# Softmax weights and an index row placed in PSUM in three edge passes of a four-layer graph network

## The reference

```python
h = jnp.maximum(_layernorm(x, axis=-1), 0.0)
x = x + _L0_gnn_ref(h, ..., node_type_4, edge_type_8, src, dst)   # typed keys, queries, values
x = x + _L1_gnn_ref(h, edge_index, ...)                            # graph attention, self loops
x = x + _L2_gnn_ref(h, src, dst, weight, bias)                     # graph convolution
x = x + _L3_gnn_ref(h, src, dst, Wq, Wk, Wv, ...)                  # clipped attention, 8 heads
```

```python
a = (kw * q_e).sum(-1) * pri / sqrt_d                 # layer 0: a dot product per edge and head
amax = jax.ops.segment_max(a, dst, num_segments=n)    # layers 0 and 1
ex = jnp.exp(a - amax[dst])
denom = jax.ops.segment_sum(ex, dst, num_segments=n)
agg = jax.ops.segment_sum(msg * att[..., None], dst, num_segments=n)
```

## Time and profile before

| | us |
|---|---|
| median of 3 runs | 10693.53 |
| lowest and highest | 10691.29, 10695.21 |
| the profiled execution | 10696.8 |
| its span, first to last instruction | 10695.1 |
| POOL busy | 7984.3 (75%) |
| PE busy | 6694.1 (63%) |
| PE weight loads | 5319.6 (50%) |
| DVE busy | 5218.1 (49%) |
| ACT busy | 2509.1 (23%) |

### The profile page before, as it was taken

The page is one execution under the profiler, slowest core; times in us unless marked ns, Lnnn a source line. Parts: engine busy times, 40 slices in busy tenths (PEclk is TensorE's granted clock), DMA queues, the critical chain, the costliest instruction groups (busy, mean ns, idle before and its releaser), DMA issues. The chain is left out here.

```text
span 10695.1 us, 165052 instructions
## 1 busy us (share of the span) xinstructions
PE 6694.1 (63%) x38290; PEld 5319.6 (50%) x38291; DVE 5218.1 (49%) x13802; ACT 2509.1 (23%) x6808; POOL 7984.3 (75%) x11114
## 2 busy tenths in 40 slices
PE   4977777777756667666663333333337777777776
PEld 3656665655535555555553232232224555555554
DVE  4266666666665555555553111111114555555555
ACT  1333333333343333333333000000002111111111
POOL 0188888888848888888865666666663888888884
PEclk9966666676765555555556555565556666666667
DMA  3333333333312212222111222222222332333332
GB/s 112 148 88 88 87 87 87 87 88 88 87 46 47 46 44 46 45 46 45 44 40 46 46 46 46 47 46 46 46 46 63 87 87 87 87 87 87 87 87 63
DMA packets 379652, 731.26 MB, mean 68 GB/s; under 512 B 169770, under 2 KB 219233, under 8 KB 373126
## 3 DMA queue, kind: packets, MB, share of 16 engines
q0 software_dynamic: 251264, 621.88, 22.1%
q1 hardware_dynamic: 100762, 97.56, 2.8%
q10 hardware_dynamic: 27500, 10.39, 0.4%
HBM read 652.50 MB, written 76.88 MB: 68 GB/s over the span
## 5 line engine op out<-in xcount | busy, mean ns | idle before, releaser
L465 POOL DMA_INDIRECT edges_rows<-conv_rows,edges_idx_r x1568 | 1536.9, 980 | 773.6 <-issue 457.9
L465 POOL DMA_INDIRECT edges_rows<-gat_rows,edges_idx_r x1568 | 1562.8, 997 | 336.1 <-issue 260.1
L465 POOL DMA_INDIRECT edges_rows<-kv_typed,edges_idx_r x1568 | 1597.6, 1019 | 267.6 <-issue 263.5
L465 POOL DMA_INDIRECT edges_rows<-kv_rows,edges_idx_r x1568 | 1522.2, 971 | 271.6 <-issue 267.7
L1022 PE MATMUL edges_ps_sum<-edges_rows,edges_pick 128*128 x3520 | 763.3, 355 | 1511.7 <-issue 1386.9
L629 PE MATMUL edges_ps_sum<-edges_wv,edges_pick 128*128 128x132 f32 x7040 | 1671.9, 409 | 20.9 <-issue 13.4
L472 POOL TENSOR_TENSOR edges_pause<-edges_pause 128x56 f32<-128x56 f32 x4704 | 1599.9, 340 | 108.1 <-issue 18.1
L629 PEld LDWEIGHTS edges_ps_sum<-edges_wv,edges_pick 128*128 128x128 f32 x7040 | 1427.0, 297 | 256.6 <-issue 246.5
L1022 PEld LDWEIGHTS edges_ps_sum<-edges_rows,edges_pick 128*128 128x128 f32 x3520 | 647.9, 257 | 1627.1 <-issue 1625.7
L1120 PE MATMUL edges_ps_q<-q,edges_pick_t 128*128 x3520 | 748.7, 379 | 674.5 <-DVE edges_prod L1184 649.7
L1042 DVE TENSOR_TENSOR sums<-sums,edges_ps_sum 128x129 f32 x440 | 126.9, 288 | 1858.5 <-DMA edges_rows<-gat_rows,edges_idx_r 1486.5
(11 more groups left out here) (345 smaller groups left out, 10934.8 us busy)
## 6 DMA issues: line engine op xcount, KB each, us to landing
kv_typed<-l0pre_out SPq DMA_DIRECT2D x49, 1024.0 KB
edges_rows<-kv_typed,edges_idx_r POOLq DMA_INDIRECT x1568
edges_rows<-gat_rows,edges_idx_r POOLq DMA_INDIRECT x1568
edges_rows<-conv_rows,edges_idx_r POOLq DMA_INDIRECT x1568
edges_rows<-kv_rows,edges_idx_r POOLq DMA_INDIRECT x1568
edges_feat_r<-visit_features ACTq DMA_DIRECT2D x660, 10.0 KB
kv_rows<-l3pre_kv SPq DMA_DIRECT2D x7, 896.0 KB
edges_flag_r<-visit_flags ACTq DMA_DIRECT2D x220, 16.0 KB
```

Of the source, the lines that this page charges most:

```text
L465: pool.indirect_dma_start(rows[:, k, g * width:(g + 1) * width], None, table, bass.IndirectOffsetOnAxis(ap=idx_r[:, k, g:g + 1], axis=0)). ...
```

## The change

It has four parts. First, DVE reads the softmax weights of `weigh` from a PSUM bank `ps_weight` in passes 0, 1 and 3. ACT writes them there with an `Exp` of its own, for the whole span in passes 0 and 1 and for the visit in pass 3, after DVE has read the weights before (`wv_done`); the `Exp` into `wv` stays, since PE sums that column. Second, in pass 0 the index row for `pick_b` is copied once into a PSUM bank `ps_iota` and read from there, as pass 3 did before. Third, the banks for this come from `ps_near`: one in place of two in pass 0, with the squares two visits ahead in place of three, and two in place of three in pass 3, with the squares three ahead in place of four. Fourth, in passes 0 and 1 `ps_turn` goes: the logits are turned, and turned back, in the first 128 columns of `ps_top`, and the maxima move up behind them. `turn_logits` therefore waits for `gap_b` of the span before, and `block_max` no longer does.

```diff
@@ -513,15 +513,16 @@
-        near_banks = 2 if dot else 1
-        ps_near = [p.ps(f"ps_near{j}", [P, GE]) for j in range(near_banks)]
+        ps_near = p.ps("ps_near", [P, GE])
...
-        ps_turn, ps_top = p.ps("ps_turn", [P, 512]), p.ps("ps_top", [P, 512])
+        ps_iota, iota_done = (p.ps("ps_iota", [P, GE]), p.sem("iota_done")) if dot else (None, None)
+        ps_top, ps_weight = p.ps("ps_top", [P, 512]), p.ps("ps_weight", [P, 512])
...
-        part9 = ps_top[:, 0:9 * SG].rearrange("p (n k) -> p n k", k=9)
-        ref8 = ps_top[:, 160:160 + 8 * SG].rearrange("p (n k) -> p n k", k=8)
+        turned_top = ps_top[:, 0:P]
+        part9 = ps_top[:, P:P + 9 * SG].rearrange("p (n k) -> p n k", k=9)
+        ref8 = ps_top[:, 288:288 + 8 * SG].rearrange("p (n k) -> p n k", k=8)
...
@@ -561,18 +562,17 @@
-                    nc.tensor.transpose(ps_turn[:, 0:P], logit[:, r, :], c["ident"]).then_inc(turn_done, 1)
+                        pe.wait_ge(gap_b, w)
+                    nc.tensor.transpose(turned_top, logit[:, r, :], c["ident"]).then_inc(turn_done, 1)
...
-                    nc.tensor.transpose(ps_turn[:, P:2 * P], run[:], c["ident"]).then_inc(back_done, 1)
+                    nc.tensor.transpose(turned_top, run[:], c["ident"]).then_inc(back_done, 1)
...
-                    if known(w, 1):
-                        pe.wait_ge(gap_b, w)
...
@@ -591,11 +591,11 @@
-                    if known(u, near_banks):
-                        pe.wait_ge(pick_tb_done, u + 1 - near_banks)
+                    if known(u, 1):
+                        pe.wait_ge(pick_tb_done, u)
...
-                    mm = nc.tensor.matmul(ps_near[s % near_banks][:], c["col_feat"], near, start=True, stop=True)
+                    mm = nc.tensor.matmul(ps_near[:], c["col_feat"], near, start=True, stop=True)
...
@@ -639,7 +639,7 @@
-                    to_square, to_spread, last, ninth = (wide_at(i, k, it, d) for d in (3 if dot else 2, 1, -1, -9))
+                    to_square, to_spread, last, ninth = (wide_at(i, k, it, d) for d in (2, 1, -1, -9))
...
@@ -656,7 +656,7 @@
-                wide_visits(pe, body, -3, 10)
+                wide_visits(pe, body, -2, 10)
...
@@ -665,6 +665,9 @@
+                        if known(u, 1):
+                            act.wait_ge(wv_done, u)
+                        nc.scalar.activation(ps_weight[:, 0:SH], gap[:, s // SPAN, :], ACT.Exp).then_inc(span_weighed, 1)
...
@@ -713,12 +716,12 @@
-                        nc.scalar.activation(pick_t[:, s % 2, :], ps_near[s % near_banks][:], ACT.Relu, bias=1.0, scale=-1.0).then_inc(pick_t_done, 1)
+                        nc.scalar.activation(pick_t[:, s % 2, :], ps_near[:], ACT.Relu, bias=1.0, scale=-1.0).then_inc(pick_t_done, 1)
...
-                    nc.scalar.activation(pick_tb[:, s, :], ps_near[s % near_banks][:], ACT.Relu, bias=1.0, scale=-1.0).then_inc(pick_tb_done, 1)
+                    nc.scalar.activation(pick_tb[:, s, :], ps_near[:], ACT.Relu, bias=1.0, scale=-1.0).then_inc(pick_tb_done, 1)
...
@@ -770,7 +773,7 @@
-                                            c["iota_bf"].unsqueeze(1).broadcast_to([P, G, P]),
+                                            ps_iota[:, 0:P].unsqueeze(1).broadcast_to([P, G, P]),
...
@@ -812,8 +815,9 @@
-                    nc.vector.tensor_tensor(wv4[:, s % 3, :, :, 0:hd], vals, bcast(wv4[:, s % 3, :, :, hd], [P, G, heads, hd]),
-                                            ALU.mult).then_inc(wv_done, 1)
+                    j = s % SPAN
+                    weights = ps_weight[:, j * GH:(j + 1) * GH].rearrange("p (g h) -> p g h", g=G)
+                    nc.vector.tensor_tensor(wv4[:, s % 3, :, :, 0:hd], vals, bcast(weights, [P, G, heads, hd]), ALU.mult).then_inc(wv_done, 1)
...
@@ -832,11 +836,11 @@
-                    nc.vector.tensor_tensor_scan(run[0:SH, :], flag_r[:, r, :], ps_turn[0:SH, 0:P], -BIG, ALU.add, ALU.max).then_inc(run_done, 1)
+                    nc.vector.tensor_tensor_scan(run[0:SH, :], flag_r[:, r, :], turned_top[0:SH, :], -BIG, ALU.add, ALU.max).then_inc(run_done, 1)
...
-                    nc.vector.tensor_tensor(ends[:], ps_turn[:, P:P + SH].rearrange("p (n h) -> p n h", h=heads),
+                    nc.vector.tensor_tensor(ends[:], turned_top[:, 0:SH].rearrange("p (n h) -> p n h", h=heads),
...
@@ -966,7 +970,9 @@
+                    nc.vector.tensor_copy(ps_iota[:, 0:P], c["iota_bf"]).then_inc(iota_done, 1)
...
+                    dve.wait_ge(iota_done, 1)
...
@@ -1068,14 +1074,15 @@
-        ps_near = [p.ps(f"ps_near{j}", [P, GE]) for j in range(3)]
+        ps_near = [p.ps(f"ps_near{j}", [P, GE]) for j in range(2)]
...
+        ps_weight = p.ps("ps_weight", [P, 512])
...
@@ -1095,9 +1102,9 @@
-                    if known(u, 3):
-                        pe.wait_ge(pick_t_done, u - 2)
-                    nc.tensor.matmul(ps_near[s % 3][:], c["col_feat"], feat_r[:, s // 2 % 3, s % 2], start=True,
+                    if known(u, 2):
+                        pe.wait_ge(pick_t_done, u - 1)
+                    nc.tensor.matmul(ps_near[s % 2][:], c["col_feat"], feat_r[:, s // 2 % 3, s % 2], start=True,
...
@@ -1122,7 +1129,7 @@
-                    to_square, to_spread, third = (wide_at(i, k, it, d) for d in (4, 1, -3))
+                    to_square, to_spread, third = (wide_at(i, k, it, d) for d in (3, 1, -3))
...
@@ -1134,7 +1141,7 @@
-                wide_visits(pe, body, -4, 4)
+                wide_visits(pe, body, -3, 4)
...
@@ -1146,6 +1153,9 @@
+                        if known(u, 1):
+                            act.wait_ge(wv_done, u)
+                        nc.scalar.activation(ps_weight[:, 0:G * heads], gap[:, s % 3], ACT.Exp).then_inc(gap_weighed, 1)
...
@@ -1155,7 +1165,7 @@
-                        nc.scalar.activation(pick_t[:, s % 2, :], ps_near[s % 3][:], ACT.Relu, bias=1.0, scale=-1.0).then_inc(pick_t_done, 1)
+                        nc.scalar.activation(pick_t[:, s % 2, :], ps_near[s % 2][:], ACT.Relu, bias=1.0, scale=-1.0).then_inc(pick_t_done, 1)
...
@@ -1189,7 +1199,8 @@
-                                            bcast(wv4[:, w, :, :, hd], [P, G, heads, hd]), ALU.mult).then_inc(wv_done, 1)
+                                            bcast(ps_weight[:, 0:G * heads].rearrange("p (g h) -> p g h", g=G), [P, G, heads, hd]),
+                                            ALU.mult).then_inc(wv_done, 1)
...
```

8 lines of the change are left out of this document (4 added, 4 removed).

## The result

The change is slower where it was first measured: 11201.41 us in the median of 4 runs (11185.15 to 11213.58) against 10694.37 for the kernel before, a ratio of 1.047 with a 95% interval of 1.0455 to 1.0485. The forecast was 10435.5. Later the same kernel was faster, 10041.85 us against 10300.83, ratio 0.9744 [0.9727, 0.976], in runs in which the kernel before was faster too. Both results hold. The experiments show what differs between the two sets of runs; what makes it differ stays open.

The account below looks back on a forecast made before the run. POOL was taken to bound passes 0 and 3, the consumers pass 1. Gains of 115 + 10 + 134 - 1 = 258 us from the median of 10693.5 gave 10435.5 us, range 10350 to 10540.

Parts of the forecast that it names:

- The stretch under L772, L815 and L1191 goes: Passes 0, 1, 3: POOL no longer stretched beside these DVE instructions; 143, 33 and 134 us of POOL time.
- A PSUM operand costs DVE nothing by itself: DVE's relieved reads: price taken as nothing, from L782 beside L1191, both 0.68 us for 512 columns.
- Parts 2, 3 and 4: Prediction's numbering: added Exp 0, up to 20 us; one bank of squares less 0; shared logits bank 0 to 20.
- POOL's time saved is time of the pass: Passes 0 and 3: POOL sets their length, so its relief shortens them, by 115 and 134 us.
- What is late next: Pass 0 after the change: consumers alone need 2238 us at 4.88 a visit plus 91, against POOL's 2260.
- The charge of 28 us: Pass 0: deducted for consumer stalls reaching POOL, between nothing and 91 us, leaving a gain of 115.
- 134 stays: Pass 3: the full 134 us gain is kept, with consumers far ahead, waiting 307 us for rows.
- the ring in pass 0: Rival, chance 0.05: with one bank, squares wait for both ACT one-hots; 6.06 us a visit, 10914 us overall.
- about 0.9 us uncovered a visit: Pass 0: the uncovered ACT time per visit from which the prediction said the ring decides.
- The gathers-not-relieved rival: Chance 0.06: long gathers only coincide with L772 and L815; at most 58 and 117 us of pauses go, 10519 us.
- The sign that was set for being wrong: Pass 0: POOL's wait for L815 appearing with more than 60 us would show the prediction wrong.
- The sum: Whole kernel: 115 in pass 0, 10 in pass 1, 134 in pass 3, less 1, gives 258 us.

Follow-up runs that it names:

- e5: The changed kernel with weigh reading its weights from SBUF again and without the added Exp and its wait; 10733.38 us, ratio 1.0048.
- e6: The changed kernel with the added Exp and its wait kept, but weigh reading the weights from SBUF; 10751.16 us, ratio 1.0056.
- e1: The kernel before with only one bank of squares less and the shorter lookahead in passes 0 and 3; 10691.25 us, ratio 1.0003.
- e2: The kernel before with only the turned logits moved to the maxima's bank, behind gap_b; 10692.32 us, ratio 1.0001.
- e3: The changed kernel with two banks of squares in pass 0 again and its index row back in SBUF; 10951.65 us, ratio 1.0232.
- e17: The changed kernel, unaltered, measured again beside the kernel before; 10041.85 us against 10300.83, ratio 0.9744.
- e18: Pass 0 of before with turned logits moved; passes 1 and 3 changed, pause 72 bf16, one-hots before Exps in pass 3; 10233.87 us, ratio 0.9934.
- e7: The changed kernel with weigh reading constant ones from PSUM and no added Exp, so values are not weighed; 11152.07 us, ratio 1.0424.
- e11: The kernel before with weigh turned into a copy reading one SBUF source, so values are not weighed; 10971.86 us, ratio 1.028.
- e10: The kernel before with POOL's pause shortened from 56 to 8 elements; 11427.72 us, ratio 1.07.
- e9: The changed kernel with POOL's pause lengthened from 56 f32 to 80 bf16 elements; 10715.4 us, ratio 1.0028.
- e13: The changed kernel with POOL's pause lengthened to 112 bf16 elements; 10723.38 us, ratio 1.0032.

## Why the prediction was wrong

Point by point:
- The stretch under L772, L815 and L1191 goes: right, to 3 ns in the pauses and 1 in the gathers of passes 0 and 3. (A pause follows each of the four gathers, 1568 of both in the earlier trace rows, and not three of the four; the sums used the right count.)
- A PSUM operand costs DVE nothing by itself: right, 676 and 680 ns for the weighing.
- Parts 2, 3 and 4 at nothing: each right on its own in the kernel before (e5 against e6, e1, e2). Part 3 is not shown to be free once the completions come later: e3 gave pass 0 two banks and 223 us back, but put the index row in SBUF as well, so the two shares stay apart only by guess.
- POOL's time saved is time of the pass: this is the step that failed. "What is late next" took the consumers' catch-up pace, 4.88 us a visit from the earlier trace rows, as their own, which no edit to POOL would touch. It was the pace under a POOL that VectorE held up twice a visit. With that gone, and completions late, pass 0 went at 2718 / 440 = 6.18 us a visit. The charge of 28 us should have been 28 + 429, by the length of pass 0. In pass 3 the same step failed: "134 stays", because the consumers were far ahead, but they held POOL for 182 us, and the pass took 2437 us for 2261. Pass 1 took 2534 for 2443.
- The rivals: the ring in pass 0 had the right symptom and the wrong cause. One bank of squares carried pass 0 at 2402 us in e1 and, with POOL relieved, at 2273 in e17. Its "about 0.9 us uncovered a visit" is also 0.68 by its own terms, since 440 x (4.88 + 0.68) + 91 = 2537 us is already 134 above 2403. None named a consumer whose completions depend on POOL. The gathers-not-relieved rival, where the rule of the Trainium skill's "SBUF — State Buffer" led, fell with the means of 961 and 959.
- The sign that was set for being wrong, over 60 us of POOL waiting for `weigh` in pass 0, came with 451.
- The sum was 258 us of gain. Where completions are prompt it was 10300.83 - 10041.85 = 259 us, with pass 0 at 2273 (forecast 2289) and pass 3 at 2262 (2261). For pass 0 the agreement can be followed: e18, in the runs beside e17, has pass 0 of before but for the turned logits, which e2 found free with completions late, and takes 2387 us there, 114 more than 2273 for a forecast of 115. For passes 1 and 3 it cannot, since the kernel before has no profile there; pass 1 went 90 us lower than forecast, from a length that is not known, so how the other 145 us divide is open.

The hint stood in the profile of before: pass 2 has no pause, and PE's sums there reached DVE 4.4 us late in the mean. The views of waits show only a part of it, since there a late completion counts only once its consumer stands ready, but they had it under "remote": 460.3 us in front of ACT's L679 in pass 0, and 425.7 us in front of DVE's L915 in pass 1.

Shown: with the pause as it was, nearly all of the loss comes with VectorE's relieved `weigh` (e5, e6, e7), and a `weigh` relieved without PSUM brings 281 us of loss too (e11); a loss appears without any relief when the pause is shortened (e10); nearly all of it goes when the pause is lengthened (e9, e13); and it is absent where PE's completions are prompt (e17). Not shown: by what path POOL's gathers hold them back, and what makes a place or a time prompt.

## What to carry to other kernels

Before you free the engine that issues indirect gathers, compare the semaphore events of PE with the modelled ends of its matmuls: if they lag by microseconds, that engine's gaps may be what lets them through, and a pace measured with the gaps says nothing of the pace without them. Try the length of the gap together with the change, since 42 ns a gather was worth 70 us of gain instead of 42 of loss in one pass. And measure such a change in more than one place and at more than one time, with the kernel before beside it: this one was 4.7% slower and 2.6% faster.

## What was unexpected of the hardware

TensorE's completions arrived microseconds after the modelled end, one in a hundred of them 13 us or more in pass 0 of after, several steps' at once, and in passes 0 and 1 of before at preferred times of the gather in progress. VectorE's came at 11 ns and ScalarE's at 8 in the same passes. The Trainium skill, "SBUF — State Buffer", section "Who interferes with whom", says that PE and ACT never wait on anyone. For their ports no run here speaks against it, but by e10 and e9 the spacing of GpSimd's gathers changes when TensorE's completions are seen, in the runs where they are late. With completions prompt, pass 2 was 268 us shorter for identical instructions, at a lower granted clock (0.52 for 0.58), so part of the time of the kernel before seems to be this lateness too. The late runs have one more mark that is not explained: the trace of before holds 36491 landing events of DMAs, that of e17 114845, for the same gathers and loads.
